# Start of an adaLN block kernel rebuilt: first batch's modulation rows by TensorE on all partitions, gates on 128 partitions, four groups half by half

## The chip, the cores and the metric

One core of a Trainium2 chip. The metric is the device time of one execution in microseconds (us). Five engines work side by side: TensorE (PE), VectorE (DVE), ScalarE (ACT), GpSimd (POOL) and SyncE (SP), which here only issues transfers.

## What is computed

x has 8 batches of 1024 tokens with 512 channels. Cut to what matters:

```python
mod = silu(c) @ wmod                      # (8, 6*512): sa, ca, ga, sb, cb, gb
ga = sign(ga) * max(|ga|, 0.25)           # the gates; gb likewise
h = layernorm(x) * (1 + ca) + sa
x = x + ga * attention(h)                 # attention output @ Wo.T + bo
h = layernorm(x) * (1 + cb) + sb
x = x + gb * ffn(h)                       # both operands quantised to FP6 in blocks of 32
```

The attention runs along axes such that only the first 16 of the 1024 tokens of each batch get a part that differs from token to token (128 "head" rows in all); for every other token it adds the row V = ga * bo. The kernel computes all tokens with x + V, and the head rows once more in full.

## The kernel before

**Tiling.** 16 groups of 512 tokens (two for each batch), each with 4 tiles of 128 tokens, so 64 tiles. The program of each engine is a loop over slots q = 0 to 63; slot q is one tile's product. Each engine's order is written out by hand: `due(q, lead)` says which group's step falls on slot q with a lead in slots, so that group g's statistics, modulation, maxima, scales and grid are made while the tiles of the groups before it are multiplied. Waits are semaphores with constants.

**A tile** (`product`, L579 to 597): TensorE turns four 128x128 blocks of the dequantised tile DD (L574), ScalarE rounds them to XH (L392), VectorE makes XL, what rounding left (L982). Then one matmul for the bias row (L587) and 12 of 512 columns: XH with the weights' high part WH (L591) and low part WL (L592), XL with WH (L596). VectorE adds the result to x (L1034), SyncE stores a group.

**A group** before that: x is loaded; V is added, on POOL for groups 0 and 1 (L320), by a DMA from DRAM that adds for the others (L313). ScalarE: sums (L419), squared deviations (L430), normalising into U (L408). POOL: times the row c = 1 + cb (L329), plus the row sb (L331). VectorE: block maxima (L1001), scales (L1006 to L1012), to the FP8 grid (L1020, two halves), back for the first half (L1027); POOL the second half (L340).

**Weights.** W is quantised once on VectorE (`quantise`, L751). For each batch POOL scales its rows by the gate (`scale_weights`, L354), TensorE turns them (L548), ScalarE and VectorE make WH (L398) and WL (L989). After the first batch one quarter is done in each of four slots (`FOLDS`).

**The start.** Six modulation products with 8 result rows, cE (8 batches) times a 512x512 piece of wmod (`modulation`, L525). The gates are computed on 8 partitions (`gate`, L773). Rows which all 128 partitions need (V, c, sb, the bias row in two parts) are written to the DRAM scratch and read back as broadcasts; ScalarE issues those of V, c and sb:

```python
act.wait_ge(v_row_done, 1)
act.dma_start(mod_dram[:, V, :], mrow[V]).then_inc(v_row_out, 16)
act.wait_ge(v_row_out, 16)
act.dma_start(v_bc[:], mod_dram[0:1, V, :].to_broadcast([P, D])).then_inc(v_in[0], 16)
```

VectorE's constants for the attention (temperatures, centred rows, centred diagonals BD at L792 to L796, rows LR at L804 and L806) all come before that. The slots of VectorE begin at -17, those of TensorE at 0.

**The head rows** (`head_work`, `attend`) ride in the slots: two norms and the modulation in slots 0 to 2, their three projections on TensorE in slots 5 to 7 (L672), three passes of attention from `BEGIN` = 8, each 15 slots, and the rest from `AFTER` = 50 on, up to slot 62.

## Time and profile before

| | |
|---|---|
| median of 3 runs | 385.32 us (383.96 to 385.49) |
| the profiled execution | 385.07 us, of which 382.8 are the span from first to last instruction |
| mean granted clock of TensorE | 0.938 of 2.4 GHz |
| busy: PE, DVE, ACT, POOL | 322.2, 290.9, 219.9, 233.8 us |
| moved by DMA | 68.10 MB, 178 GB/s on average |

Rows of the page give, for a group of like instructions, where in the kernel they stand (L591), engine, operation, what is written from what, shape and count, then busy time and the mean of one in ns, then the idle time of the engine just before them and what ended it. "PEclk" is the share of 2.4 GHz that TensorE was granted; 0.5 is its lower level of 1.2 GHz.

### The profile page before, as it was taken

The page shows a single profiled execution, that of the slowest core. Times are in us where ns is not written, and L with a number is a line of the kernel's source. Part 1 is how long each engine was busy: PE and PEld are TensorE (multiplying, and loading weights), DVE is VectorE, ACT ScalarE, POOL GpSimd, SP SyncE. Part 2 cuts the span into 40 slices and gives each one's busy share as a digit, 9 for nine tenths or more (in the row PEclk, how much of TensorE's full clock was granted, in tenths as well). Part 3 has the DMA queues.
Part 4 walks back from the last instruction along what each step waited for, and adds up shares of the span by engine and source line. Part 5 has one row for each costly group of instructions (what it writes and reads, how often), then busy time and mean ns, then how long its engine had stood idle before and what let it go on. Part 6 is the DMA issues. An engine that isn't in the chain of part 4 may idle for free.

```text
span 382.8 us, 6288 instructions
## 1 busy us (share of the span) xinstructions
PE 322.2 (84%) x2302; PEld 245.4 (64%) x2302; DVE 290.9 (76%) x500; ACT 219.9 (57%) x498; POOL 233.8 (61%) x139
## 2 busy tenths in 40 slices
PE   2950065886899999999999998989999999995994
PEld 0100012664799887778888776878887878674883
DVE  2893397598764698498969877999886799799533
ACT  2001858483755787688695968767874877120310
POOL 2004886929969569675995887596956693800100
PEclk9995569589999999999999999999998999999999
DMA  7998355869874966678486939684966971102032
GB/s 262 388 406 332 96 74 197 142 196 308 200 176 87 300 106 225 100 288 158 172 176 211 217 118 239 176 197 141 242 161 167 222 165 68 45 0 110 33 133 82
DMA packets 23156, 68.10 MB, mean 178 GB/s; under 512 B 2563, under 2 KB 2692, under 8 KB 19022
## 3 DMA queue, kind: packets, MB, share of 16 engines
q1 hardware_dynamic: 14982, 51.67, 37.9%
q0 software_dynamic: 7392, 14.68, 24.8%
q10 hardware_dynamic: 752, 1.36, 1.1%
q8 instruction: 18, 0.29, 0.3%
q14 instruction: 12, 0.10, 0.1%
HBM read 50.50 MB, written 17.20 MB: 177 GB/s over the span
## 4 chain that ended last, share of the span: by engine, by line
PE 49%; DVE 22%; issue 8%; ACT 7%; POOL 7%; DMA 4%; SPq 1%; DVEq 0%; POOLq 0%; ACTq 0%
PE ps L591 9%; PE ps L592 9%; PE ps L596 9%; PE ps L574 5%; PE ps L548 3%; DVE XL L982 3%; PE ps L672 3%; PE ps L587 3%; DMA v_bc<-mod_scratch 2%; POOL U L329 2%; POOL U L331 2%; DVE amax L1001 2%; DVE WL L989 2%; DVE X L1034 1%; PE ps L603 1%
## 5 line engine op out<-in xcount | busy, mean ns | idle before, releaser
L591 PE MATMUL ps<-WH,XH 128*128 128x512 f32 x256 | 103.0, 402 | 0.7 <-ACT XH L392 0.7
L592 PE MATMUL ps<-WL,XH 128*128 128x512 f32 x256 | 102.6, 401 | 0.0
L329 POOL TENSOR_TENSOR U<-U,c_bc 128x1024 f32<-128x1024 f32 x32 | 78.3, 2447 | 31.6 <-ACT U L408 31.6
L392 ACT ACTIVATE XH<-ps 128x512 fp32r<-128x512 f32 x64 | 37.9, 593 | 86.2 <-PE ps L574 86.1
L331 POOL TENSOR_TENSOR U<-U,sb_bc 128x1024 f32<-128x1024 f32 x32 | 76.8, 2398 | 2.5
L982 DVE TENSOR_TENSOR XL<-ps,XH 128x512 fp32r<-128x512 f32 x64 | 44.0, 688 | 45.1 <-ACT XH L392 42.5
L596 PE MATMUL ps<-WH,XL 128*128 128x512 f32 x256 | 69.7, 395 | 1.0 <-DVE XL L982 1.0
L408 ACT ACTIVATE U<-X,nmr,rstd 128x512 f32<-128x512 f32 x64 | 48.6, 810 | 21.0 <-DVE nmr L997 21.0
L592 PEld LDWEIGHTS ps<-WL,XH 128*128 128x128 f32 x256 | 49.5, 193 | 11.4
L419 ACT ACTIVATE unused<-X 128x512 bf16<-128x512 f32 x64 | 39.5, 620 | 29.6 <-POOL X L320 27.7
L596 PEld LDWEIGHTS ps<-WH,XL 128*128 128x128 f32 x256 | 48.5, 190 | 12.2 <-DVE XL L982 1.7
L591 PEld LDWEIGHTS ps<-WH,XH 128*128 128x128 f32 x256 | 49.8, 194 | 10.0 <-ACT XH L392 1.2
L1034 DVE TENSOR_TENSOR X<-ps,X 128x512 f32<-128x512 f32 x64 | 43.7, 682 | 9.9 <-PE ps L596 9.8
L340 POOL TENSOR_TENSOR DD<-Q,s 128x1024 f32<-128x1024 fp8e4 x16 | 30.7, 1916 | 32.8 <-DVE Q L1020 25.4
L430 ACT ACTIVATE unused<-X,negm 128x512 bf16<-128x512 f32 x64 | 45.6, 717 | 0.5
L1001 DVE TENSOR_REDUCE amax<-U 128x32 f32<-128x1024 f32 x32 | 38.7, 1211 | 4.8 <-POOL U L331 4.8
L574 PE MATMUL ps<-idf,DD 128*128 128x128 f32 x256 | 40.2, 283 | 0.2 <-POOL DD L340 0.2
L1020 DVE TENSOR_TENSOR Q<-U,ps 128x1024 fp8e4<-128x1024 f32 x32 | 39.0, 1218 | 0.6
L574 PEld LDWEIGHTS ps<-idf,DD 128*128 128x128 f32 x256 | 31.6, 146 | 3.2 <-issue 1.1
L587 PE MATMUL ps<-G,onesr 128*128 128x512 f32 x64 | 31.3, 489 | 0.9 <-DVE X L1034 0.9
L313 POOL DMA_DIRECT2D X<-mod_scratch x14 | 18.1, 1294 | 18.8 <-DMA X<-in_x 18.8
L320 POOL TENSOR_TENSOR X<-X,v_bc 128x1024 f32<-128x1024 f32 x4 | 9.2, 2341 | 31.4 <-DMA v_bc<-mod_scratch 31.4
(211 smaller groups left out, 441.8 us busy)
## 6 DMA issues: line engine op xcount, KB each, us to landing
X<-in_x SPq DMA_DIRECT2D x16, 1024.0 KB, 4.9
out<-X SPq DMA_DIRECT2D x15, 1024.0 KB, 7.6
X<-mod_scratch POOLq DMA_DIRECT2D x14, 1024.0 KB, 11.6
X<-in_wmod SPq DMA_DIRECT2D x4, 1024.0 KB, 9.4
c_bc<-mod_scratch SPq DMA_DIRECT2D x6, 256.0 KB, 9.9
sb_bc<-mod_scratch SPq DMA_DIRECT2D x6, 256.0 KB, 9.8
Wd<-in_w SPq DMA_DIRECT2D x1, 1024.0 KB, 12.7
U<-in_wmod SPq DMA_DIRECT2D x1, 1024.0 KB, 14.8
```

The costliest lines, as they stand in the source:

```text
L329: nc.gpsimd.tensor_tensor(a, a, spread(c_bc[:, b % 2, :]), ALU.mult).then_inc(u_done, 1)
L331: nc.gpsimd.tensor_tensor(a, a, spread(sb_bc[:, b % 2, :]), ALU.add).then_inc(h_done, 1)
L408: A.activation(U[:, g % 2, j, :], X1[:, g % XSLOTS, j, :], ACT.Identity, bias=nmr[:, g % 2, j:j + 1], scale=rstd[:, g % 2, j:j + 1]).then_ ...
L430: A.activation(unused[:, j % 2, :], X1[:, g % XSLOTS, j, :], ACT.Square, bias=negm[:, g % 2, j:j + 1], accum_out=ss[:, j:j + 1]).then_inc( ...
L574: m = TR(ps[:, XT_BANK + n % 2, c * P:(c + 1) * P], DD[:, j, c * P:(c + 1) * P], idf[:])
L587: M(bank, onesr[:], G2[:, b % 2, :], start=True, stop=False)
L591: M(bank, XH[:, n % 2, r], WH[:, b % 2, k, :], start=False, stop=False)
L592: M(bank, XH[:, n % 2, r], WL[:, b % 2, k, :], start=False, stop=False)
L596: m = M(bank, XL[:, n % 2, r], WH[:, b % 2, k, :], start=False, stop=k == NC - 1)
L982: TT(XL[:, n % 2, :], ps[:, XT_BANK + n % 2, :], XH[:, n % 2, :].bitcast(F32), ALU.subtract).then_inc(xl_done, 1)
L1001: RED(amax[:, h, :], blocks(U[:, g % 2, HALF * h:HALF * (h + 1), :]), AX, ALU.max, apply_absolute_value=True).then_inc(am_done, 1)
L1034: TT(a, ps[:, Y_BANK + n % 2, :], a, ALU.add).then_inc(o_done, 1)
```

## The change

What it does, part by part:

- **V.** TensorE makes the first batch's ga row on all 128 partitions at once (`spread`): the weights are one column of cE repeated 128 times. VectorE forms V from it with a broadcast of bo (`first_v`) and adds it to group 0 itself; POOL adds it to group 1. The c and sb rows of batch 0 come the same way; ScalarE copies them out of PSUM.
- **Gates.** Their 8 rows are turned into 128 partitions x 32 (4 chunks of 8 batches); the gate is computed there, and times bo and the bias as columns. Four blocks are turned back into 32 rows (gate-bias, V, gb, ga for 8 batches) and written to DRAM by one DMA. The bias row of a product is now picked out of G by the weights `pick`, so that no load for each batch is needed.
- **Head modulation.** ca and sa come from two products with 128 result rows in slots 0 and 1 (`head_rows`), read from PSUM; before, 8 broadcast loads.
- **Groups 0 to 3** (`FILLING`) are treated half by half, and both halves of DD are made by VectorE; their steps have slots of their own. The steps of group 0 stand before the loop.
- **Moved.** LR rows to slot 1 and BD's centring to slot 4 on VectorE; the product for the c rows of all batches to slot 0 on TensorE; head projections to slots 6 to 8, `BEGIN` to 9, `AFTER` to 51; the folds of batch b to slots 8b-5 to 8b-2.
- **Loads** are in another order: the first piece of wmod in two halves, the identity second, W before the second piece, BD and the head's x late. Three small loads go to ScalarE's queue. The DMA addition of V for group g+3 is issued after group g's modulation.

```diff
 def fold_slot(b, k):
-    return k if b == 1 else 56 + k if b == B else 8 * b - 8 + (0, 1, 4, 5)[k]
+    return 56 + k if b == B else 8 * b - 5 + k
...
+        NORMAL = {2: (3, 3), 3: (6, 6), 4: (8, 9)}
+        DEVIATE = {2: (2, 2), 3: (5, 5), 4: (7, 7)}
+        SUM = {2: (1, 1), 3: (4, 4), 4: (5, 6)}
+        FILLING = 3
...
             sp.dma_start(cTs[:], cT.rearrange("(k p) b -> p k b", p=P)).then_inc(c_loaded, 16)
-            load_mod(0)
+            sp.dma_start(idf[:], ident).then_inc(small_in, 16)
+            load_mod(0, 0, HALF)
+            load_mod(0, HALF, NC)
+            sp.dma_start(bo_bc, bo[None, :].to_broadcast([P, D])).then_inc(bo_in, 16)
             load_x(0)
+            sp.dma_start(Wd[:], w.rearrange("(c p) k -> p c k", p=P)).then_inc(w_in, 16)
             load_mod(1)
+            load_x(1)
             load_mod(2)
-            sp.dma_start(Wd[:], w.rearrange("(c p) k -> p c k", p=P)).then_inc(w_in, 16)
             load_mod(3)
-            load_x(1)
+            load_x(2)
+            sp.wait_ge(columns_cp, 1)
+            sp.dma_start(mod_dram[0:COLUMNS].rearrange("w b d -> (w b) d"), column_rows).then_inc(columns_out, 16)
...
         @block.gpsimd
+            add_attn_bias(1)
+            scale_weights(0, Wfirst, 0, HALF)
+            scale_weights(0, Wfirst, HALF, NC)
+            modulate(0)
+            sum_by_dma(2)
+            scale_weights(1, Wsecond)
+            sum_by_dma(3)
...
         @block.tensor
+            def spread(i, bank, signal):
+                for k in range(NC):
+                    pe.wait_ge(wmod_in[6 if i == 0 and k < HALF else i], 16)
+                    m = M(ps[:, bank, :], cE[:, k, 0:1].to_broadcast([P, P]), mod_w[i][:, k, :],
+                          start=k == 0, stop=k == NC - 1)
+                m.then_inc(signal, 1)
...
-                M(bank, onesr[:], G2[:, b % 2, :], start=True, stop=False)
+                M(bank, pick[:, b:b + 1].to_broadcast([P, P]), G[:], start=True, stop=False)
...
+                if q == 0:
+                    pe.wait_ge(c_heads, 1)
+                    pe.wait_ge(wt_low, NC)
+                    pe.wait_ge(rows_cp, 3)
+                    rows_of(2, LATE_ROWS)
+                    head_rows(4, CA_BANK)
+                elif q == 1:
+                    head_rows(5, SA_BANK)
...
         @block.vector
+            early_constants()
+            first_v()
+            dve.wait_ge(w_in, 16)
+            quantise(Wd[:, 0:HALF, :], Q8[:, 0], HALF * NB).then_inc(wd_done, 1)
+            gate(0, GA, BO, V, dve_step)
...
+            gate(1, GB, BIAS, GBIAS, gb_col)
+            scales(0)
+            quantise(Wd[:, HALF:NC, :], Q8[:, 1], HALF * NB).then_inc(wd_done, 1)
+            gate_bias_rows()
+            first_modulate()
+            maxima(0, 0)
+            block_scales(0, 0, 1)
+            to_grid(0, 0)
+            from_grid(0, 0)
+            for k in range(NC):
+                weight_low(0, k, W_FIRST_BANKS[k])
+            low_part(0)
```

Where the orders of the engines show it, with each instruction's semaphores. First TensorE at the start of the program, before (8x512 is a modulation with 8 result rows, L561 the gate turned, L548 the weights turned):

```order
L528 MATMUL ps<-X,cE 8x512 [waits wmod_in0,silu_done]
L555 MATMUL ps<-ones,lrow 128x1 [waits rows_ok,cleared]
L528 MATMUL ps<-X,cE 8x512 [waits wmod_in1]
L528 MATMUL ps<-X,cE 8x512 [waits wmod_in2]
L528 MATMUL ps<-U,cE 8x512 [waits wmod_in3]
L561 MATMUL ps<-idf,early 128x8 [waits gb_row,small_in]
L528 MATMUL ps<-X,cE 8x512 [waits wmod_in4,blq_cp]
L528 MATMUL ps<-Wb,cE 8x512 [waits wmod_in5,gb_cp]
L548 MATMUL ps<-idf,X 128x128 [waits mod_cp,wscaled]
```

and after (L589 is `spread`, L596 a modulation with 8 rows, L602 a gate turned, L639 the gate columns turned back, L623 the weights turned):

```order
L589 MATMUL ps<-X,cE 128x512 [waits wmod_in6,silu_done]
L589 MATMUL ps<-X,cE 128x512 [waits wmod_in0] x2
L596 MATMUL ps<-X,cE 8x512 [waits wmod_in0]
L602 MATMUL ps<-idf,msp 128x8 [waits rows_cp,small_in]
L596 MATMUL ps<-X,cE 8x512 [waits wmod_in1]
L602 MATMUL ps<-idf,msp 128x8 [waits rows_cp]
L589 MATMUL ps<-X,cE 128x512 [waits wmod_in2] x4
L639 MATMUL ps<-idf,TA 32x128 [waits gb_col]
L589 MATMUL ps<-U,cE 128x512 [waits wmod_in3] x4
L596 MATMUL ps<-U,cE 8x512 [waits wmod_in3,blq_cp]
L623 MATMUL ps<-idf,Wb 128x128 [waits g_rows,wscaled,columns_cp,v_row]
```

Three products with 128 result rows and two turns of the gates have come in; two of the six modulations have left for slots 0 and 1.

VectorE, after, from V on to the first turn's input (before, these steps lie in slots -17 to -2, with V and the gates on 8 partitions):

```order
L906 SCALAR_TENSOR_TENSOR v_bc<-odd,ps 128x512 [waits dve_step]
L911 TENSOR_TENSOR X<-X,v_bc 128x1024 [waits x_in0,v_row]
L862 TENSOR_REDUCE ps<-Wd 128x32 [waits w_in]
L890 TENSOR_SCALAR gate_sign<-ps 128x32 [waits gate_mm]
L1119 RECIPROCAL ps<-sd 128x4 [waits sd_done]
L917 CAST G<-ps 8x512 [waits columns_cp,cleared]
L959 SCALAR_TENSOR_TENSOR U<-ps,U 128x1024 [waits c_rows,z_done]
L962 TENSOR_TENSOR U<-U,ps 128x1024 [waits s_rows,u_first]
L1129 TENSOR_REDUCE amax<-U 128x32 [waits h_first]
L1155 TENSOR_TENSOR DD<-Q,ps 128x1024 [waits q_done]
L1114 TENSOR_TENSOR WL<-ps,WH 128x512 [waits wt_high] x4
L1107 TENSOR_TENSOR XL<-ps,XH 128x512 [waits xh_done]
```

The addition of V and the modulation of group 0's first half have moved from POOL to VectorE, and the low parts of the weights now stand behind the first half of DD.

## Rows read from the trace of the kernel before

**Rows 1.** The page, part 2: TensorE busy and its clock, in tenths

```profile
PE   2950065886899999999999998989999999995994
...
PEclk9995569589999999999999999999998999999999
```

**Rows 2.** Table by stage (us, busy us of each engine, clock, DMA share, GB/s)

```profile
0.00:69.02 69.02, 29.89 (x78) 8.88 (x78) 45.07 (x90) 27.84 (x68) 31.32 (x28) 0.78 0.75 250
69.02:128.31 59.29, 51.15 (x286) 42.63 (x285) 40.77 (x71) 33.45 (x81) 45.93 (x26) 0.91 0.77 192
128.31:374.80 246.49, 238.12 (x1931) 191.68 (x1930) 203.62 (x337) 158.58 (x350) 156.54 (x87) 0.99 0.59 157
374.80:382.80 8.00, 3.10 (x14) 2.24 (x12) 1.38 (x2) 0.00 (x0) 0.00 (x0) 1.00 0.31 98
...
80.00:90.00 10.00, 6.43 (x32) 4.82 (x30) 9.72 (x18) 5.07 (x14) 4.05 (x3) 1.00 0.88 291
```

**Rows 3.** Chain of waits before the first product (start us, us, what)

```profile
22.34 4.24 DMA mod_scratch<-early
26.60 7.60 DMA v_bc<-mod_scratch
...
36.63 2.35 POOL X L320
...
53.53 2.72 DVE XL L833
```

**Rows 4.** Timeline of TensorE: slot starts (start us, us, instruction)

```profile
69.02 0.79 PE L587 MATMUL ps<-G,onesr 128*128 128x512 f32 x1
...
98.02 0.48 PE L587 MATMUL ps<-G,onesr 128*128 128x512 f32 x1
...
128.31 0.48 PE L587 MATMUL ps<-G,onesr 128*128 128x512 f32 x1
```

**Rows 5.** Timeline of TensorE: modulation products

```profile
6.86 5.59 PE L528 MATMUL ps<-X,cE 128*8 128x512 f32 x8 [6.86 <-DMA X<-in_wmod]
...
21.43 3.60 PE L528 MATMUL ps<-U,cE 128*8 128x512 f32 x8 [1.09 <-DMA U<-in_wmod]
```

**Rows 6.** Groups of instructions by line (busy us, mean ns of one)

```profile
L329 POOL TENSOR_TENSOR U<-U,c_bc 128x1024 f32<-128x1024 f32 x32 | 78.3, 2447 | 31.6 <-ACT U L408 31.6
...
L408 ACT ACTIVATE U<-X,nmr,rstd 128x512 f32<-128x512 f32 x64 | 48.6, 810 | 21.0 <-DVE nmr L997 21.0
...
L982 DVE TENSOR_TENSOR XL<-ps,XH 128x512 fp32r<-128x512 f32 x64 | 44.0, 688 | 45.1 <-ACT XH L392 42.5 <-PE ps L596 2.5
...
L1020 DVE TENSOR_TENSOR Q<-U,ps 128x1024 fp8e4<-128x1024 f32 x32 | 39.0, 1218 | 0.6
L1001 DVE TENSOR_REDUCE amax<-U 128x32 f32<-128x1024 f32 x32 | 38.7, 1211 | 4.8 <-POOL U L331 4.8
...
L1027 DVE TENSOR_TENSOR DD<-Q,ps 128x1024 f32<-128x1024 fp8e4 x16 | 19.4, 1212 | 0.0
...
L354 POOL TENSOR_SCALAR Wb<-Wd,gbTs 128x512 f32<-128x512 f32 x24 | 16.2, 687 | 3.9 <-PE ps L672 3.9
...
L320 POOL TENSOR_TENSOR X<-X,v_bc 128x1024 f32<-128x1024 f32 x4 | 9.2, 2341 | 31.4 <-DMA v_bc<-mod_scratch 31.4
```

**Rows 7.** Timeline of VectorE: BD and LR constants

```profile
11.80 0.27 DVE L792 TENSOR_REDUCE bdm<-BD 128x1 f32<-128x128 f32 x1
...
17.00 0.68 DVE L806 TENSOR_TENSOR LR<-lrow,LR 1x512 fp32r<-1x512 f32 x1
```

**Rows 8.** Timeline of TensorE around its first slots [idle before]

```profile
66.52 1.09 PE L548 MATMUL ps<-idf,X 128*128 128x128 f32 x4 [4.68 <-DVE WL L989]
...
75.33 2.08 PE L596 MATMUL ps<-WH,XL 128*128 128x512 f32 x4 [1.03 <-DVE XL L982]
...
81.30 1.07 PE L596 MATMUL ps<-WH,XL 128*128 128x512 f32 x4
```

**Rows 9.** Timeline of TensorE: a head projection

```profile
104.54 3.73 PE L672 MATMUL ps<-sq,early 128*128 128x128 f32 x32
```

**Rows 10.** The page, part 6: DMA additions

```profile
X<-mod_scratch POOLq DMA_DIRECT2D x14, 1024.0 KB, 11.6
```

**Rows 11.** Timeline of POOL: a wait for x of group 3

```profile
85.87 1.29 POOL L313 DMA_DIRECT2D X<-mod_scratch  x1 [7.61 <-DMA X<-in_x]
```

More of the change, by code:

```diff
@@ L24, with build @@
 XSLOTS = 6
-V, C, SB, GB, GBIAS, CA, SA, GA, GBH, GBL = range(10)
-FIRST, LAST = -17, TILES * GROUPS
-BEGIN, PERIOD = 8, 15
-AFTER = 36 + 14
+GBIAS, V, GB, GA, C, SB = range(6)
+COLUMNS, ROWS = 4, 6
+LAST = TILES * GROUPS
+BEGIN, PERIOD = 9, 15
+AFTER = BEGIN + 2 * PERIOD + 12
 def fold_slot(b, k):
-    return k if b == 1 else 56 + k if b == B else 8 * b - 8 + (0, 1, 4, 5)[k]
+    return 56 + k if b == B else 8 * b - 5 + k
 FOLDS = {fold_slot(b, k): (b, k) for b in range(1, B + 1) for k in range(NC)}
-def build(nc, x, xh, WqT, WkT, WvT, WoT, bo, lna, BDs, rows, columns, masks, w, bias, cT, wmod, ident, out):
-    mod_dram = nc.dram_tensor("mod_scratch", (B, 10, D), F32, kind="Internal").ap()
+def build(nc, x, xh, WqT, WkT, WvT, WoT, bo, lna, BDs, rows, columns, masks, w, cT, wmod, ident, out):
+    mod_dram = nc.dram_tensor("mod_scratch", (ROWS, B, D), F32, kind="Internal").ap()
     xg = x.rearrange("b (g p j) d -> (b g) p j d", p=P, j=TILES)
@@ L183, in due, with additions, halves @@
             return g if r == 0 and 0 <= g < GROUPS else None
-        def mods(i):
-            return ps[0:B, (0, 1, 2, 3, 6, 7)[i], :]
+        def additions(g):
+            return g // XSLOTS + (g % XSLOTS >= 2)
+        NORMAL = {2: (3, 3), 3: (6, 6), 4: (8, 9)}
+        DEVIATE = {2: (2, 2), 3: (5, 5), 4: (7, 7)}
+        SUM = {2: (1, 1), 3: (4, 4), 4: (5, 6)}
+        def halves(q, early, lead):
+            done = [(g, h) for g, slots in early.items() for h in range(2) if slots[h] == q]
+            for h in range(2):
+                g = due(q, lead - h)
+                if g is not None and g > 4:
+                    done.append((g, h))
+            return done
+        FILLING = 3
         def pass_of(q):
@@ L374, in _ @@
             A = nc.scalar
+            act.dma_start(col[:], columns).then_inc(vec_in, 16)
+            act.dma_start(lrow[:], rows).then_inc(vec_in, 16)
+            act.dma_start(mk[:], masks).then_inc(mk_in, 16)
             act.wait_ge(c_loaded, 16)
@@ L411, in sums @@
             def sums(g, h):
[L412 to L413 removed]
+                if g == 0:
+                    act.wait_ge(v_row, h + 2)
+                elif g == 1:
+                    act.wait_ge(x1_done, h + 1)
                 else:
[L415 removed]
+                    act.wait_ge(x_added[g % XSLOTS], 16 * additions(g))
                 for j in range(HALF * h, HALF * (h + 1)):
@@ L511, in _ @@
                     weight_high(*FOLDS[q - 1], W_BANK)
+                if q == 0:
+                    deviations(1, 1)
+                    for h in range(2):
+                        normalise(1, h)
                 head_work(q)
-                for h in range(2):
-                    if (g := due(q, 9 - h)) is not None:
-                        normalise(g, h)
-                    if (g := due(q, 11 - h)) is not None:
-                        deviations(g, h)
-                    if (g := due(q, 13 - h)) is not None:
-                        sums(g, h)
+                if q == 1:
+                    copy_rows(c_rows_all, LATE_ROWS, 4, 1.0)
+                for g, h in halves(q, NORMAL, 9):
+                    normalise(g, h)
+                for g, h in halves(q, DEVIATE, 11):
+                    deviations(g, h)
+                for g, h in halves(q, SUM, 13):
+                    sums(g, h)
         @block.tensor
```

626 lines of the change are left out of this document (345 added, 281 removed).

## The prediction

> **What bounds the kernel now.** I read four views, in this order. The page's slices [rows 1] show where TensorE works: low and broken digits in the first seven or eight slices of 9.6 us, then mostly nines. The table by stage [rows 2] says it in numbers: before the first product, 69.02 us in which TensorE is busy for 29.89; then nine token tiles (slots 0 to 8, one product each) in 59.29 us; then 246.49 us with TensorE busy for 238.12 of them, at a granted clock of 0.99; the last slot and the tail take 8 us. A slot's floor on TensorE is the 3.43 us from 98.02 to 101.45 [rows 4] (a turn and one product with nothing beside them), so nine slots at the floor would take 31 us where these take 59. The change touches the first 128.31 us, and all it can save lies there.
>
> The chain of waits [rows 3] names what fills the first 69 us: the row v is written to DRAM (4.24 us) and read back on all partitions (7.60 us); POOL then adds it to tokens; DVE computes the second gate on 8 partitions after group 0's statistics, and at 53.53 rounds its bias row in a 2.72 us instruction of 8 partitions; POOL scales the weights; TensorE turns them. The slot starts [rows 4] are the measure that I carry over: 69.02, 98.02 (slot 4, the first of group 1) and 128.31 (slot 9).
>
> **Times at the new start, step by step.** I lay the new program's orders against the durations of rows, and look for when slot 0 starts.
>
> Loads. TensorE's first modulation starts when 1 MB is in, at 6.86; the one that starts at 21.43 waits for a load with 5.6 MB more in front [rows 5], so 0.385 MB/us or 2.7 us for each MB. The first half of the first weight piece is then in at about 5.7, the second at 7, x of group 0 at 10.5, W at 13.2, piece 2 at 16, x of group 1 at 18.6, piece 3 at 21.4, piece 4 at 24, x of group 2 at 27.
>
> TensorE. One modulation product with 512 columns costs 5.59 us when it begins at half rate and 3.60 at full rate [rows 5], 3.44 when the next follows at once. I take the same for 128 result rows as for 8, because in both the 512 columns are what streams. So: v on all partitions 5.7 to 11.5, gate rows 14.9, the first gate turned 16.3, piece 2 19.7, the second gate turned 21.3 (it waits for ScalarE, busy with deviations until 20.1 and then with the copy), the c rows 24.8, the four turns of the gate columns 25.4, sb rows 28.9, batch rows of sb 32.3, the turned weights 34.3.
>
> VectorE. v from 11.5 to 14.3 (four operations of 512 columns at 0.69), the two additions of group 0 to 16.7 (I take 1.2 each, as for L1020; POOL takes 2.45 for such an operation [rows 6]), half of W quantised to 21.0 (three passes over 1024 columns at 1.22 and two small ones), both gates to 23.6 (twelve operations of 32 columns, 0.2 each), the other half of W to 28.4, the bias rows 29.8, c and sb applied to half of group 0 32.3, maxima, scales, grid and back to 36.5, four low parts of the weights 39.1 [rows 6]. ScalarE's share beside it: sums and deviations of group 0 from 15.5 to 22.6, then its normalisation waits until 26.0 behind the copy of the turned gate columns, which itself waits for TensorE until 25.4; that wait is hidden, as VectorE is in W until 28.4. POOL's four weight scalings (0.69 each) end at 29.8, hidden too.
>
> Slot 0 therefore starts at about 39.1 in place of 69.02, with VectorE as the engine that sets it: 29.9 us earlier. Removed with it are the DRAM round trip of v and c (11.84 us of the chain) and the slow 8-partition operations on two SBUF operands beside POOL.
>
> On the round trip a page can be weighed. The rows give 4.24 and 7.60 us [rows 3], with loads of 1 MB in front of it in the same engines. The Trainium skill ("DMA: Bandwidth & Descriptors", section "Anatomy of one DMA") gives about 2.0 us fixed plus the bytes at 436 GB/s, an estimate of 2.0 and 2.6 us for these two; by that the removal would be worth 4.6 us and not 11.8. The trace disagrees, and my sum uses the new chain's own steps, so it doesn't hang on either.
>
> **The filling, slots 0 to 8.** What moves in: the batch rows of c and both head modulations, three products of 3.44 us on TensorE in slots 0 and 1 (10.3 us); on VectorE the centring of BD and the LR rows, which ran in 11.80 to 17.68 before [rows 7] (5.2 us without the two small ones), now in slots 1 and 4; and for groups 0 to 3 the second half of DD, 1.2 us a group, which POOL did.
>
> The clock: after an idle of 4.68 us TensorE's operations ran at half level from 66.52; four product steps at 75.33 took 2.08 us against 1.07 at 81.30 [rows 8]. The new start has a similar pause (34.3 to 37.9). I take half level for about 12.5 us as in the rows: the product of slot 0 costs 5.5, and the first moved modulation 2.8 more than at full rate.
>
> Then by hand, with the same durations and those 2.8 left out until the end: slot 0 from 39.1 to 44.7; two modulations to 51.6; slot 1 to 55.3; the third to 58.8; slot 2 to 62.8; slot 3 to 66.3; slot 4 at 67.8. There VectorE is behind: in slot 2 it must do 1.2 + 1.2 + 0.5 for group 1 and 3.6 for the head's second norm, in slot 4 3.0 for BD, beside 1.4 in every slot for the output addition and XL. So slot 5 is at 74 and slot 6 at 79; then slots 6, 7 and 8 are 7.5 us each, since TensorE has a head projection of 3.73 [rows 9] beside the floor and a weight turn: slot 7 at 86.4, slot 8 at 94, slot 9 at 100.9, and 103.7 with the 2.8. An operation of 512 columns that need not wait for the one before takes 0.60 in a row of them, as the piece at 45.06 [rows 3], and not 0.69; some 30 of these in the filling take 2.5 us off: 101.2. POOL (four passes of 2.4 us a group, 9.7 in about 17) keeps up.
>
> The DMA addition for group 5 now comes after group 2's modulation, at about 81, and by the row lands 11.6 us later [rows 10], at 93, when ScalarE would want it from about 90. I take 0 for it, since ScalarE's next urgent step is slot 9's, and keep 3 us for the upper end.
>
> **After slot 9.** Before, this is 254.5 us (128.31 to 382.80). The attention chain begins one slot later, so its first step (two products of 512 columns and four small ones, 1.9 us) now lies behind slot 9, and one more weight turn does, 0.4. The rest of the rhythm is the same: TensorE is busy 97% there. The folds are now in four slots in a row (8b-5 to 8b-2), before in slots 0, 1, 4, 5 of eight, whose VectorE share is heaviest (two grid passes); I take 0 between bounds of -3 and +3.
>
> Sum: 101.2 + 1.9 + 0.4 + 254.5 = 358.0 of span. The profiled execution was 385.07 with a span of 382.8, so 2.3 is added: 360.3, a gain of 24.8 on 385.07, which is 0.25 below the median of 385.32. A measurement of this kernel can tell about 0.5%, 1.9 us, from no change.
>
> **Rivals.**
> - *VectorE gives most of the filling back.* The moved constants and the head's norm delay XL, which delays every product; VectorE does 40.77 of 59.29 us in the filling before [rows 2] and gets about 9 more. If the moved work (10.3 on TensorE, 5.2 on VectorE, 3.6 for DD) hides nowhere, slots 0 to 8 take the old 59.3 plus 19.1 in place of 62.1: 377. Half of it hidden gives 367. Against it: the old 59.3 already holds pauses for weights and x.
> - *The start itself is late.* VectorE's list is in order, and it has about ten waits for other engines before slot 0, which I count at nothing; at 0.9 us each slot 0 starts at 48: 369. Against it: in the chain the read of v follows its write with nothing between (22.34 + 4.24 and 26.60) [rows 3], so the hops of the old start are small.
> - *Filling at TensorE's pace.* If VectorE's work fits beside it: 39.1 + 9 × 3.43 + 10.3 + 7.3 for two projections before slot 8's end, 3.7 for the third, and 1.7 of turns is 93: 352. For it: the old filling holds pauses that the new one need not have, as POOL's 7.61 us for x of group 3 [rows 11], whose load is issued earlier now.
> - *Slower: TensorE stays at half level through the filling and beyond.* Its place is the gaps that VectorE leaves in every slot; a product step then costs 0.43 and not 0.23, so a slot at least 3.0 us more. From 9 such slots on the 24.8 us are gone; 12 give 396. For it: half level lasted from 66.52 to 79 though TensorE was mostly busy. Against it: in the ten us behind, it was busy for only 6.43 and had full level throughout [rows 2].
>
> **How the numbers follow.** The forecast, 360.3, has 0.60; VectorE giving back (367) 0.15; the late start (369) 0.10; TensorE's pace (352) 0.12; slower (396) 0.03. The range goes from 350 to 372: below it takes in the third rival and -3 for the folds, above the first two with 3 us for ScalarE's wait. Faster by over 0.5%: 0.96; within: 0.01; slower: 0.03.
>
> **What would show it.** The first product's start at 37 to 42; v ready on all partitions by 15 with no DMA in its chain; no TensorE idle over 5 us after 6 us; slot 4 at 66 to 72, slot 9 at 98 to 104; from there on the same 250 to 258 us. Wrong would be a first product after 45, a span after slot 9 beyond 260, or a granted clock near 0.5 after slot 3.

## The result: 370.37 us, a gain of 14.8 where 24.8 were forecast

| | before | changed |
|---|---|---|
| median | 385.19 us | 370.37 us (369.68 to 372.18, 4 runs) |
| ratio | | 0.9628, 95% interval 0.9585 to 0.9672 |
| the profiled execution, span | 385.07, 382.8 | 371.03, 369.1 |
| slot 0 starts | 69.02 | 39.44 |
| slots 0 to 8 take | 59.29 | 68.31 |
| from slot 9 to the end of the span | 254.49 | 261.35 |

The kernel is faster, inside the range, and 10 us slower than the centre. The page of the changed kernel, its slices and its chain, against [rows 1]:

```profile
PE   3987999549999799989999999989999989995894
...
PEclk9999899997999999999999999999998999998999
...
PE 43%; DVE 36%; ACT 10%; issue 8%; DMA 1%; DVEq 0%; SPq 0%; ACTq 0%
```

Seven or eight slices of low digits before slot 0 and in the filling have shrunk to a few: after the first slice (of 9.2 us) come 9, 8, 7 and nines. A 5 and a 4 remain in the eighth and ninth slices (65 to 83 us), with a 7 in the clock right behind them. VectorE holds 36% of the chain that ended last. The table by stage, against [rows 2] (us from:to, length, busy us of PE, PEld, DVE, ACT, POOL, clock, DMA share, GB/s):

```profile
0.00:39.44 39.44, 28.32 (x86) 11.59 (x87) 30.54 (x70) 19.83 (x45) 18.70 (x23) 0.97 0.92 325
39.44:107.75 68.31, 58.64 (x296) 44.36 (x294) 52.24 (x91) 42.93 (x108) 38.56 (x22) 0.94 0.81 211
107.75:361.10 253.35, 240.70 (x1946) 193.46 (x1943) 206.60 (x345) 160.28 (x353) 159.66 (x88) 0.99 0.60 154
361.10:369.10 8.00, 3.10 (x14) 2.25 (x12) 1.39 (x3) 0.00 (x0) 0.00 (x0) 0.95 0.32 98
```

Before slot 0 TensorE does about what it did (28.32 us against 29.89), in 39 us instead of 69. Behind, both stages are longer than before. The chain of waits before the first product, against [rows 3] (start, us, what), has no transfer in it after the first piece of wmod:

```profile
1.79 4.29 DMA X<-in_wmod
...
6.21 5.50 PE ps L589 x8
...
14.00 0.70 DVE v_bc L906
14.72 2.36 DVE X L911 x2
...
28.21 0.68 DVE G L917
28.95 0.68 issue
29.63 1.23 DVE U L959
...
36.57 1.21 DVE WL L1114 x2
...
37.82 1.97 PE ps L660 x8
```

And the slot starts on TensorE's timeline (L675 is the bias row, L623 a weight turn; [idle before]), against [rows 4]:

```profile
39.44 0.78 PE L675 MATMUL ps<-G,pick 128*128 128x512 f32 x1
...
43.13 3.60 PE L596 MATMUL ps<-X,cE 128*8 128x512 f32 x8
...
66.64 0.50 PE L675 MATMUL ps<-G,pick 128*128 128x512 f32 x1 [0.65 <-DVE X L1162]
...
74.39 0.48 PE L675 MATMUL ps<-G,pick 128*128 128x512 f32 x1
...
82.96 0.45 PE L623 MATMUL ps<-idf,odd 128*128 128x128 f32 x1 [5.33 <-DVE WL L1114]
...
84.55 0.78 PE L675 MATMUL ps<-G,pick 128*128 128x512 f32 x1
...
107.75 0.47 PE L675 MATMUL ps<-G,pick 128*128 128x512 f32 x1
```

Slot 4 is at 66.64 and slot 5 at 74.39, where the forecast had 67.8 and 74 before it added its 2.8 us for half level at the start. Those 2.8 us were never paid: behind TensorE's pause before slot 0 the granted clock is 0.5 only until about 40.5, and the first moved modulation, at 43.13, runs at full rate. Then slot 6 is at 84.55 (79 forecast), and TensorE idles 5.33 us in front of it, waiting for VectorE. After that pause the same bias row takes 0.78 us and not 0.48: half level again. VectorE's timeline says what held it:

```profile
72.75 0.68 DVE L1114 TENSOR_TENSOR WL<-ps,WH 128x512 fp32r<-128x512 f32 x1
73.34 0.27 DVE L948 TENSOR_REDUCE bdm<-BD 128x1 f32<-128x128 f32 x1
73.65 0.15 DVE L949 TENSOR_SCALAR bdm<-bdm 128x1 f32<-128x1 f32 x1
73.84 5.19 DVE L952 TENSOR_SCALAR BD<-BD,bdm 32x32 f32<-32x32 f32 x4
...
79.58 1.19 DVE L952 TENSOR_SCALAR BD<-BD,bdm 32x32 f32<-32x32 f32 x4
...
80.93 0.69 DVE L1162 TENSOR_TENSOR X<-ps,X 128x512 f32<-128x512 f32 x1
```

and POOL's, over the same stretch:

```profile
74.07 2.39 POOL L370 TENSOR_TENSOR U<-U,c_bc 128x1024 f32<-128x1024 f32 x1
76.60 2.39 POOL L377 TENSOR_TENSOR U<-U,sb_bc 128x1024 f32<-128x1024 f32 x1
```

Four subtractions on 32x32 elements, the centring of BD, take 5.19 us, and end at 79.03, when POOL's modulation ends (78.99). The next four, with POOL's modulation over, take 1.19. One by one (the view of line L952: shortest, median and longest in ns), most take 0.23 to 0.27 us, and the one that starts at 74.17, just behind the start of a POOL pass, takes 2.32, about a whole pass:

```profile
L952 DVE TENSOR_SCALAR BD<-BD,bdm x8: 229/270/2320, 73.8 to 80.5; 32x32 f32<-32x32 f32 x8
```

The pair that starts at 76.53 takes 2.50, so two such waits and two ordinary subtractions make the 5.19 us. Not every VectorE instruction beside POOL waits: the sum at 73.34 and the 128x1 product at 73.65 have both ends in SBUF as well and take the 0.27 and 0.15 us that they took before.

In the kernel before the subtractions stood at 12.29, and POOL had no instruction there; that row lies between the two of [rows 7], from which the 3.0 us were sized (timeline of VectorE, kernel before):

```profile
12.29 1.03 DVE L796 TENSOR_SCALAR BD<-BD,bdm 32x32 f32<-32x32 f32 x4
```

The slower price could have been read in the kernel before. The same step of the gate there (L779, on 8 partitions, SBUF to SBUF) stands once where POOL is silent and once beside POOL's first modulation pass (46.07 to 48.41):

```profile
19.75 0.41 DVE L779 TENSOR_SCALAR hs<-hs 8x512 f32<-8x512 f32 x1
...
46.40 2.29 DVE L779 TENSOR_SCALAR hs<-hs 8x512 f32<-8x512 f32 x1
```

The prediction also uses two rows of the kernel before that it does not show. The piece at 45.06 in the chain of waits, and the slot start at 101.45 on TensorE's timeline, are these:

```profile
45.06 0.60 DVE hs L777
```

```profile
101.45 0.48 PE L587 MATMUL ps<-G,onesr 128*128 128x512 f32 x1
```

So the missing 10 us are mainly in two places: slots 5 and 6, 19.4 us where 12.4 were forecast, and slots 10 to 15, 30.8 us where the kernel before took 27.1. The rest is spread thinly over slots 16 to 63.

### The profile page after: what moved, and what is told of

Its sections match the earlier page's. It is cut to its first block, busy times and chain, and to the rows that moved or that the text cites. A ratio compares the mean times of both kernels' runs of the same rounds, so it can differ in the third digit from the quotient of the medians.

```text
span 369.1 us, 6369 instructions
## 1 busy us (share of the span) xinstructions
PE 330.8 (90%) x2334; PEld 251.7 (68%) x2334; DVE 290.8 (79%) x508; ACT 223.0 (60%) x505; POOL 216.9 (59%) x131
## 4 chain that ended last, share of the span: by engine, by line
PE 43%; DVE 36%; ACT 10%; issue 8%; DMA 1%; DVEq 0%; SPq 0%; ACTq 0%
PE ps L679 7%; PE ps L680 7%; PE ps L684 7%; DVE XL L1107 5%; PE ps L660 4%; DVE Q L1148 4%; DVE WL L1114 3%; DVE amax L1129 3%; ACT U L447 3%; PE ps L763 3%; DVE X L1162 3%; PE ps L623 3%; DVE DD L1155 3%; ACT XH L430 2%; ACT unused L460 2%
## 5 line engine op out<-in xcount | busy, mean ns | idle before, releaser
L370 POOL TENSOR_TENSOR U<-U,c_bc 128x1024 f32<-128x1024 f32 x31 | 75.6, 2439 | 48.3 <-ACT U L447 48.2
L430 ACT ACTIVATE XH<-ps 128x512 fp32r<-128x512 f32 x64 | 37.8, 591 | 84.8 <-PE ps L660 84.6
L377 POOL TENSOR_TENSOR U<-U,sb_bc 128x1024 f32<-128x1024 f32 x31 | 74.1, 2389 | 4.5 <-POOL U L370 0.2
L684 PE MATMUL ps<-WH,XL 128*128 128x512 f32 x256 | 68.8, 390 | 0.0
L460 ACT ACTIVATE unused<-X 128x512 bf16<-128x512 f32 x64 | 39.4, 617 | 0.1
L356 POOL TENSOR_TENSOR DD<-Q,s 128x1024 f32<-128x1024 fp8e4 x12 | 23.0, 1916 | 23.4 <-DVE Q L1148 21.8
L675 PE MATMUL ps<-G,pick 128*128 128x512 f32 x64 | 31.3, 490 | 0.6 <-DVE X L1162 0.6
L346 POOL DMA_DIRECT2D X<-mod_scratch x14 | 18.5, 1325 | 17.5 <-DMA X<-in_x 12.7
L389 POOL TENSOR_SCALAR Wb<-Wd,TA 128x512 f32<-128x512 f32 x28 | 18.9, 691 | 12.8 <-PE ps L623 8.3
## 6 DMA issues: line engine op xcount, KB each, us to landing
X<-mod_scratch POOLq DMA_DIRECT2D x14, 1024.0 KB, 12.8
```

Of the source, the lines that this page charges most:

```text
L370: nc.gpsimd.tensor_tensor(a, a, spread(c_bc[:, b % 2, :]), ALU.mult).then_inc(u_done, 2 if g == 0 else 1)
L377: nc.gpsimd.tensor_tensor(a, a, spread(sb_bc[:, b % 2, :]), ALU.add).then_inc(h_done, 2 if g == 0 else 1)
L460: A.activation(unused[:, j % 2, :], X1[:, g % XSLOTS, j, :], ACT.Identity, accum_out=total[:, j:j + 1]).then_inc(sum_done, 1)
L684: m = M(bank, XL[:, n % 2, r], WH[:, b % 2, k, :], start=False, stop=k == NC - 1)
```

## The experiments

Each ratio is against the kernel before on the same chip. The table gives where the time lay, in us, from TensorE's slot starts; "5+6" is slot 5's start to slot 7's, "10-15" slot 10's to slot 16's.

| kernel | ratio [95%] | slot 0 at | 5+6 | slots 0-9 | 10-15 | 10-62 |
|---|---|---|---|---|---|---|
| before | 1 | 69.02 | 14.0 | 64.0 | 27.1 | 241.8 |
| changed | 0.9628 [0.9585, 0.9672] | 39.44 | 19.4 | 73.7 | 30.8 | 248.0 |
| changed, again | 0.9610 [0.9567, 0.9654] | 40.08 | 17.7 | 73.1 | 30.7 | 247.4 |
| no_centre | 0.9484 [0.9428, 0.9540] | 41.24 | 12.3 | 67.6 | 32.3 | 249.3 |
| centre_act | 0.9472 [0.9402, 0.9543] | 41.38 | 12.8 | 67.2 | 30.8 | 246.5 |
| centre_q1 | 0.9600 [0.9543, 0.9657] | 41.29 | 11.3 | 68.9 | 32.4 | 252.7 |
| warm | 0.9693 [0.9639, 0.9747] | 41.25 | 16.8 | 71.2 | 30.7 | 250.5 |
| fold_old | 0.9701 [0.9655, 0.9748] | 41.58 | 19.4 | 74.5 | 29.9 | 247.7 |
| b_shift | 1.0026 [0.9995, 1.0057] | 68.98 | 14.0 | 62.8 | 27.4 | 244.2 |
| swap | 0.9645 [0.9605, 0.9684] | 40.0 | 17.5 | 72.7 | 32.3 | 249.3 |
| centre_act_swap | 0.9517 [0.9468, 0.9566] | 40.42 | 11.3 | 65.6 | 32.3 | 249.2 |
| a_shift10 | 0.9537 [0.9496, 0.9579] | 40.31 | 17.6 | 70.6 | 28.4 | 247.6 |
| centre_act_shift10 | 0.9392 [0.9357, 0.9427] | 40.20 | 11.3 | 63.7 | 28.4 | 246.5 |
| roundtrip | 1.0009 [0.9975, 1.0043] | 53.01 | 19.7 | 74.0 | 30.7 | 247.8 |

The ratio rests on 4 to 10 runs of each kernel; the slots are those of the one execution that was profiled, and for no_centre and centre_q1 that was the slowest (367.99 and 372.92 us, medians 365.81 and 369.63). Some of the table moves without an edit. With the same program up to slot 0 it starts at 39.4 to 41.6. Slot 13 takes 5.4 us in both executions of the changed kernel, in centre_act, warm and roundtrip, and 6.9 to 7.0 in no_centre, centre_q1, swap and centre_act_swap, whose edits do not touch it. In the two executions of the changed kernel slots 32 to 39 take 36.5 and 38.1 us, and slots 32 to 47 together 73.4 and 72.8.

The changed kernel once more, on the chip of centre_q1, b_shift and roundtrip:

> The changed kernel once more, beside the three others of this call, as their common base: 370 to 373 us. In the last call slot 0 started at 41.2 to 41.6 in four kernels whose start is the same program as here, where it was 39.44; there the second piece of wmod came in at 18.1 and TensorE waited. If that is the run and not the kernel, this one too may start anywhere from 39.4 to 41.6.

It came at 370.38 us: the difference between the two kernels repeats. The four subtractions take 5.18 us there and again end with POOL's pass.

### The centring of BD: left out, given to ScalarE, or moved to slot 1

Without the subtractions (no_centre; this kernel leaves the centring out, so its attention is not the right one):

```diff
-                    for q in range(4):
-                        r = slice(32 * q, 32 * q + 32)
-                        link(TS(BD[r, i, r], BD[r, i, r], bdm[r, n:n + 1], None, ALU.subtract))
```

> BD is not centred (the eight 32x32 subtractions of L952 are left out, so the logits use uncentred projections); the rest of the changed kernel is as it was. Theory A: these eight small instructions cost VectorE 6.4 us in slot 4 because the first four sat behind POOL's modulation (5.19 us against 1.03 us for the other kernel), TensorE idled 5.3 us for it and came back at half rate; then slots 5 and 6 (10.16 and 9.21 us) fall to about 5 and 7.5, and the time falls by 5 to 8 us, to 362 to 365. Rival B: VectorE is behind in the filling anyway (its list for groups 1 and 2), and the wait reappears in slots 5 to 7: under 2 us, 368 to 370.

Measured 365.81 us (364.46 to 367.99), ratio 0.9484, 0.8 us above theory A's range and 2.2 below rival B's; slots 5 and 6 fell from 19.4 (17.7 in the repeat) to 12.3, close to the 12.4 of the forecast.

The eight subtractions on ScalarE (centre_act), while VectorE keeps only the sums and means:

```diff
+                elif q == 6:
+                    act.wait_ge(bd_mean, 2)
+                    for n, i in enumerate((0, 2)):
+                        for j in range(4):
+                            r = slice(32 * j, 32 * j + 32)
+                            A.activation(BD[r, i, r], BD[r, i, r], ACT.Identity, bias=bdm[r, n:n + 1]
+                                         ).then_inc(bd_done, 1)
```

> The same centring, but the eight 32x32 subtractions are done by ScalarE in slot 6 (as an addition of minus the mean), VectorE keeps only the sums and means. Theory A (VectorE's two-sided small instructions wait for POOL): ScalarE's take 0.2 us each also while POOL modulates, 1.6 us in all in a slot where it idles, so the gain is that of leaving them out, within 1 us: 362 to 366. Rival B: any engine's access slows beside POOL, then these eight take over 0.5 us each and XH of slot 7 is late: 367 or more.

Measured 366.61 us (363.49 to 369.44), ratio 0.9472, slots 5 and 6 in 12.8. ScalarE's timeline of this kernel, and that of POOL beside it:

```profile
83.93 2.70 ACT L520 ACTIVATE BD<-BD,bdm 32x32 f32<-32x32 f32 x8
```

```profile
80.82 1.28 POOL L346 DMA_DIRECT2D X<-mod_scratch  x1
```

Eight take 2.70 us, 0.34 each where 0.2 was expected, in about the place where VectorE needed 5.19 + 1.19. POOL's next modulation starts at 88.33, so this run does not show how ScalarE fares beside it, and does not decide between theory A and rival B; it shows that the work costs next to nothing there. Computing all and leaving the centring out give the same time within their intervals: the loss in slots 5 and 6 was this step on VectorE.

The same subtractions on VectorE, at the end of its slot 1 (centre_q1):

```diff
                 elif q == 1:
                     bias_rows()
+                    centre_diagonals()
...
-                elif q == 4:
-                    centre_diagonals()
```

> The centring of BD stays on VectorE, with the same instructions, but moves from slot 4 to the end of slot 1, where POOL has nothing between 57.6 and 69.2. Theory A: each group of four small instructions takes 1.03 us there, as in the kernel before, not 5.19; slots 5 and 6 fall to 12 to 13 us together from 19.4, slots 1 to 3 grow by up to 3: a gain of 3 to 6 us on the changed kernel of this call. Rival: the slowness belongs to the instructions (32 partitions, 32 columns) or to VectorE's place in the order, then slot 1 grows by 6 and nothing is gained.

VectorE's timeline of this kernel; POOL's last instruction there had ended at 59.41:

```profile
60.91 1.04 DVE L952 TENSOR_SCALAR BD<-BD,bdm 32x32 f32<-32x32 f32 x4
...
62.49 1.04 DVE L952 TENSOR_SCALAR BD<-BD,bdm 32x32 f32<-32x32 f32 x4
```

Same engine, same instructions, 1.04 us where they took 5.19: what makes them slow is POOL's work beside them. Slots 5 and 6 fell to 11.3. But the time fell only to 369.63, 0.8 us under the changed kernel beside it where 3 to 6 were expected: slots 1 to 3 grew by 4.1 to 4.8 (expected up to 3). The profiled execution, 3.3 us above the median, also has longer slots 10 to 15 and 32 to 39. Of this kernel's expected gain only the local part came.

### TensorE kept busy through the pause

```diff
+                elif q == 5:
+                    for n in range(20):
+                        M(bb, onesr[:], LR[:, 0, :], start=True, stop=True)
```

(Nothing reads these 20 products.)

> Twenty matmuls of 512 columns with no use are put on TensorE behind slot 5's product, into a PSUM bank that is free there; the centring stays on VectorE. They fill 4.6 of the 5.3 us in which TensorE idles at 77.6 to 83. Theory C: of the loss in slots 5 and 6 about 2 to 3 us are the half rate that follows the idle; slot 6 falls from 9.21 to about 7 and the time by 2 us, to 368. If the half rate cost nothing (VectorE was late for slot 7 anyway), the time stays at 370 to 371, with slot 7 starting where it did.

TensorE's timeline of warm:

```profile
79.24 4.72 PE L784 MATMUL ps<-LR,onesr 128*128 128x512 f32 x20
84.77 0.30 PE L623 MATMUL ps<-idf,odd 128*128 128x128 f32 x1 [0.80 <-DVE WL L1117]
...
85.58 0.47 PE L675 MATMUL ps<-G,pick 128*128 128x512 f32 x1
```

The bias row takes 0.47 instead of 0.78, and slot 6 takes 7.43 instead of 9.21. From the first turn behind the pause to slot 7 it is 8.24 us (84.77 to 93.01) against 10.80 (82.96 to 93.76). So the half level after the pause cost 2.5 us of those 19.4; in the repeat of the changed kernel, where the same stretch takes 9.84, it cost 1.6. The total did not fall: it is 373.42 us, 3 more than the changed kernel. In the profiled executions 1.8 of that is a later slot 0 (41.25 against 39.44), which the edit does not touch, and slots 32 to 39 took 39.3 against 36.5 and 38.1. The expected gain of the whole is a miss, and only the local one stands.

### The folds where they were before

```diff
-    return 56 + k if b == B else 8 * b - 5 + k
+    return 56 + k if b == B else k + 3 if b == 1 else 8 * b - 8 + (0, 1, 4, 5)[k]
```

> The weight folds of batches 2 to 7 go back to slots 8b-8 + (0, 1, 4, 5); nothing else. The stretch behind slot 10 takes 6.2 us longer in the changed kernel than in the one before. Theory D: the folds in four slots in a row cause it (VectorE's two grid passes and the fold in the same slot): then 3 to 6 us come back, 364 to 367. Rival E: it is the attention chain, shifted by one slot against the groups' rhythm: then under 1.5 us either way, 369 to 372.

Measured 374.45 us, ratio 0.9701, above the ranges of both theories. Slots 10 to 62 take 247.7 against 248.0 us, with slots 10 to 15 0.9 shorter. Four folds in a row are not what made the later part longer. At the old places the kernel is about 4 us slower; in the profiled executions half of that is a later slot 0 (41.58 against 39.44), before any of these folds, so how much the folds cost is not shown.

### The attention one slot later in the kernel before

```diff
-BEGIN, PERIOD = 8, 15
+BEGIN, PERIOD = 9, 15
...
-AFTER = 36 + 14
+AFTER = 37 + 14
```

(with the two steps behind `AFTER` that would leave the last slot drawn in by one.)

> The kernel before, with the attention passes begun one slot later (BEGIN 9, AFTER 51, the last two steps of the head rows in the same slots as before): nothing else. Theory E: the attention chain, one slot later against the groups' four-slot rhythm, puts its heavy VectorE steps on slots that are already heavy; then slots 10 to 63 take 3 to 6 us longer than the 241.8 us of the kernel before, and the time rises to 388 to 391. Rival: the stretch is longer in the changed kernel for another reason (order on POOL, the four folds in a row); then this stays at 384.5 to 386.5.

Measured 386.31 us, ratio 1.0026, inside the rival's range; slots 10 to 15 in 27.4 against 27.1. The shift by itself does not cost the 3.7 us. This kernel has the attention in the same slots as the changed one, so it is the better measure for them: slot by slot the changed kernel is longer by 2.45 us in slot 12 (6.33 against 3.88), by 0.5 in slots 11 and 14 each, and within 0.05 in the three others.

### V through DRAM again

```diff
+            act.dma_start(v_dram, v_first[0:1, :]).then_inc(wv_in, 16)
+            act.wait_ge(wv_in, 16)
+            act.dma_start(v_bc[:], v_dram.to_broadcast([P, D])).then_inc(wv_in, 16)
...
-                STT(v_bc[:], gate_tmp, 2.0, m, ALU.mult, ALU.mult).then_inc(v_row, 1)
+                STT(v_first[:], gate_tmp, 2.0, m, ALU.mult, ALU.mult).then_inc(bd_done, 1)
+                dve.wait_ge(wv_in, 32)
```

> In the changed kernel VectorE's row V goes out to DRAM from one partition (2 KB) and comes back as a broadcast to 128 partitions (256 KB) before anything uses it, as in the kernel before; all else stays. By the rows of the kernel before (4.24 and 7.60 us behind the loads) slot 0 starts 10 to 12 us later and the time rises by about as much, to 381 to 384. By the page's 2.0 us and 2.6 us it is 4.6 us: 375 to 377. Rival: VectorE takes no step while it waits, so nothing hides it; only if the quantising of W were moved into the wait would it be less.

Measured 385.74 us, ratio 1.0009 [0.9975, 1.0043]: this one step takes the whole gain of the change back, more than the 381 to 384 that were expected. Slot 0 starts at 53.0, 12.9 us later than in the changed kernel beside it. The chain of waits of this kernel, and what VectorE waits for on its timeline:

```profile
14.26 0.69 DVE v_first L912
14.95 10.21 issue
...
25.26 4.52 DVE X L919 x2
```

```profile
25.17 0.06 DVE L914 MEMSET dn<- 128x1 f32 x1 [10.22 <-DMA v_bc<-v_scratch]
```

VectorE stands for 10.21 us, close to the 11.84 that [rows 3] gave and far from the 4.6 that was estimated from the Trainium skill ("DMA: Bandwidth & Descriptors", "Anatomy of one DMA"). That section of the Trainium skill gives its figures for a transfer that GpSimd's queue issues. Here ScalarE issues both (at 15.04 and 19.07), so the 4.6 us were borrowed from another path, and neither this run nor [rows 3] is a test of them. The two additions behind it now coincide with POOL's own on group 1 and take 4.52 us instead of 2.36; POOL's two take 6.67 where they took 4.67. That is 10.2 + 2.2 of the 12.9 us.

### The order of loads

```diff
-            sp.dma_start(Wd[:], w.rearrange("(c p) k -> p c k", p=P)).then_inc(w_in, 16)
             load_mod(1)
+            sp.dma_start(Wd[:], w.rearrange("(c p) k -> p c k", p=P)).then_inc(w_in, 16)
```

> Only the order of the two loads changes, the centring stays in slot 4. Theory: 0 to 1.5 us under the changed kernel's 370.4, slot 0 at 39 to 40, with slots 5 and 6 at 17.7 to 19.4 together as before.

> Centring on ScalarE as in centre_act, and the second piece of wmod is loaded before W and not behind it. The second piece is then in 2.7 us earlier (15.4 at the latest instead of 18.1), before TensorE is free for it at 16.3, and W 2.7 us later at worst at 18, against VectorE's need at 17. Theory: slot 0 starts at 39 to 40 in every execution and not at 41.2, and the time is 364 to 366, 4.5 to 6 us under the changed kernel's 370.4. Rival: W comes in late at 18 and more and the start only swaps one wait for another; then slot 0 stays at 41 and the time at centre_act's 366.6.

Neither shows a gain: swap 371.82 us (0.9645 against 0.9610 for the changed kernel, intervals that overlap; 368.9 to 370.4 were expected), centre_act_swap 366.06 (0.9517 against 0.9472). Slot 0 starts at 40.0 and 40.4, inside the range that it has without the edit, so one execution of each decides nothing about the start.

### The attention one more slot later in the changed kernel

```diff
-BEGIN, PERIOD = 9, 15
+BEGIN, PERIOD = 10, 15
```

> The changed kernel with the attention passes begun in slot 10 and not 9; nothing else. Slots 10 to 16 take 30.8 us in the changed kernel and 27.1 in the one before; a shift of that one by a slot left them at 27.4. Theory F: VectorE has no gap between 114.2 and 133.8 there because the attention's norm steps of pass 0 (slots 11 and 12) meet group 3's steps, which are half by half and all on VectorE; one slot later they meet group 4's lighter slot, and slots 10 to 16 change by over 1 us either way. Rival G: the load of VectorE is simply more than these slots hold, wherever the steps stand; then slots 10 to 17 stay within 1 us of the same sum, and the time at 369 to 373.

Measured 367.73 us, ratio 0.9537, under the 369 to 373 of rival G. Slots 10 to 15 fell from 30.8 to 28.4, as theory F had it. But most of that is where the count begins and ends. The attention's first step has left slot 9 (5.40 us before the shift, 3.42 behind it) for slot 10, and a slot of 7.0 us has moved from 15 to 16. From slot 10 to slot 17, the stretch that rival G names, it is 35.5 against 34.7 us, within G's 1 us, so that only the time speaks against G. Over slots 9 to 16, which take in both moves, it is 38.9 against 40.1 us, 1.2 less. Slots 16 to 31 take 74.5 where they took 71.6, and slots 10 to 62 as long as before (247.6 against 248.0 and 247.4). From slot 9 to slot 63 the gain is 1.8 us against the repeat and 2.3 against the first execution. What fills slots 10 to 15 shows in the table by stage over just these six slots, of the kernel before,

```profile
133.03:160.14 27.11, 27.11 (x258) 21.22 (x257) 21.21 (x39) 19.83 (x46) 19.90 (x13) 1.00 0.62 148
```

of the changed kernel, with its slot 12,

```profile
121.28:127.61 6.33, 4.04 (x25) 3.20 (x23) 6.09 (x13) 6.01 (x14) 4.19 (x2) 1.00 0.74 168
...
113.15:143.91 30.76, 28.48 (x242) 22.62 (x240) 26.18 (x45) 21.48 (x50) 21.43 (x14) 1.00 0.56 131
```

and of a_shift10:

```profile
110.95:139.39 28.44, 27.06 (x154) 22.52 (x152) 27.10 (x47) 20.28 (x49) 20.46 (x13) 1.00 0.59 147
```

The third busy figure is VectorE's: 21.21 us before, 26.18 after. In slot 12 TensorE stands for 2.3 of 6.33 us. On its timeline VectorE has no gap from 114.2 to 137 us of the changed kernel. A piece of it:

```profile
121.61 1.22 DVE L1155 TENSOR_TENSOR DD<-Q,ps 128x1024 f32<-128x1024 fp8e4 x1
122.75 1.21 DVE L1129 TENSOR_REDUCE amax<-U 128x32 f32<-128x1024 f32 x1
123.88 0.68 DVE L989 TENSOR_REDUCE ps<-sq 128x16 f32<-128x512 f32 x1
...
125.37 0.68 DVE L1107 TENSOR_TENSOR XL<-ps,XH 128x512 fp32r<-128x512 f32 x1
```

and TensorE's next turn of a weight:

```profile
126.79 0.63 PE L623 MATMUL ps<-idf,Wb 128*128 128x128 f32 x4 [2.29 <-DVE WL L1114]
```

TensorE waits here for WL, the fold's low part (125.96 to 126.64), which stands right behind XL; both stand behind two passes of 1.2 us and the attention's norm. Over the six slots VectorE makes three DD passes where it made one, three grid passes instead of two, five maxima instead of four, and one more low part: four passes, 1.1 us each from start to start, and one of 0.6 account for the 5.0 us more that it is busy. In a_shift10 VectorE has as much to do (27.10 us) and 1.3 us of gaps instead of 4.6, and TensorE's waits for WL there are 0.67 and 0.71 us instead of 2.29. So in slot 12 VectorE, full, makes TensorE stand, and where the attention's norm falls among its passes changes by about 0.9 us what is lost. Nothing was run with less work on VectorE in these slots, so that its extra passes cause the 3.4 us is argued from the wait and the busy times and not shown.

### Both edits together

```diff
-BEGIN, PERIOD = 9, 15
+BEGIN, PERIOD = 10, 15
```

on centre_act.

> The two edits that each made the changed kernel faster, in one kernel: the subtractions on ScalarE (ratio to the kernel before 0.947 alone) and the work between slots begun one slot later (0.954 alone; the changed kernel itself 0.961). Theory H: they remove different waits, the first VectorE's stall beside GpSimd in slot 5, the second a part of the full VectorE in slots 10 to 16. Then slots 5 to 7 stay near 12 us and slots 10 to 16 fall from 31 to 28 or 29, and the ratio is 0.934 to 0.943 (360 to 363 us against 385). Theory I: both only give VectorE room in the same stretch, slots 4 to 16, and what the first gives the second cannot give again; then the ratio is that of the first alone, 0.944 to 0.952, and slots 10 to 16 stay at 30 or more.

Measured 362.08 us (360.39 to 363.39, 6 runs), ratio 0.9392 [0.9357, 0.9427]: every number of theory H came. Its page:

```profile
PE   3889799779999899989999999889999997995994
...
PEclk9999899999999999999999999999999999999898
```

Slots 5 and 6 take 11.3 us, slots 10 to 15 28.4. The two gains do add, but H's reason for the second is not borne out: slots 10 to 62 take 246.5 us as in centre_act, and what the shift gives lies in slot 9 (3.43 against 5.41). The rest between these two profiled executions is a slot 0 that starts 1.2 us earlier and slots 5 and 6, 11.3 against 12.8, which the shift does not touch. Slot 9 starts at 100.4, where the forecast had 101.2, and the time is 1.8 us above the forecast. This is the fastest of all kernels here.

## Why the prediction was right, and 10 us too good

**The start, right.** Slot 0 was put at 39.1 and came at 39.44; V was ready at 14.7 (forecast 14.3), the two additions of group 0 ended at 17.08 (16.7), W's second half at 28.3 (28.4), the four low parts of the weights at 38.96 (39.1); TensorE starts to turn the tiles when two of them are there, at 37.8. The chain named VectorE as the engine that sets it, which it is. The rival of a late start is out.

**The round trip, right by the row.** The sum has no term for it, as the new chain has no such step, but the prediction said that 11.84 us go with it. Put back, it makes VectorE stand for 10.21 us and the kernel 15.4 us slower than the changed kernel beside it (385.74 us against 370.38).

**The filling up to slot 4, right, and in part by luck.** Slot 4 came at 66.64 (67.8, or 70.6 with the 2.8), and no wait for the group 5 addition was found on the path. But "half level for about 12.5 us as in the rows" did not come: it lasted 2.7 us from TensorE's first instruction behind the pause, at 37.82. Slot 0's product took 3.7 us and not 5.5, and the 2.8 for the first moved modulation were not paid. Without these 4.6 us the forecast has slot 9 at 96.6, and 107.75 is then 11 us late and not 6.5. The sum's error is so much larger than its result shows: 7.0 in slots 5 and 6, 1.6 in slot 4 (7.75 us against 6.2), and the 2.5 us taken off for operations that need not wait, which no slot shows by itself.

**"In slot 4 3.0 for BD" failed.** The step sized it from [rows 7], where POOL is silent, and slot 4 lies where POOL modulates. It took 7.6 us, from 73.34 to 80.9; TensorE idled 5.33 us for it and resumed at half level (2.5 us by warm). Slots 5 and 6 took 19.4 us and not 12.4, which alone is more than the error of the filling (68.3 against 62.1), and no_centre, centre_act and centre_q1 each remove it. The prediction itself spoke of "slow 8-partition operations on two SBUF operands beside POOL" as something that the change removes, and did not ask which new ones it puts there. Nor are two SBUF operands needed: the subtraction reads one tensor and a column of means, and L779 of the kernel before reads a single tensor (0.41 us against 2.29). The Trainium skill has the rule ("SBUF — State Buffer", section "Terms"): VectorE and GpSimd arbitrate for one port pair, exclusive for a full instruction, and the loser blocks altogether. The trace agrees for these subtractions: single ones of 2.32 us, as long as a pass, and 5.19 us for four that end with POOL's pass, against 1.04 with POOL idle. It does not bear it out for every VectorE instruction: the sum of 0.27 us at 73.34 ran beside a pass.

**"The rest of the rhythm is the same" failed.** After slot 9 the sum added 2.3 us to 254.5, and 261.4 were measured. Against b_shift, which has the attention in the same slots, 3.4 us more lie in slots 10 to 15, 2.45 of them in slot 12. The sum charged the 1.2 us a group for DD's second half to slots 0 to 8 alone, and the table by stage shows VectorE with 5.0 us more in slots 10 to 15, where it has no room. It never asked what VectorE does in the slots in which the last half-by-half group and the attention's first norm meet. The folds, 0 between -3 and +3, are confirmed at 0 for the later part.

**VectorE gives back filling** (367, 0.15) was the rival nearest to what happened, but not for its reason: it was not the sum of the moved work, but one small step with a wait in it, and a full stretch behind slot 9. TensorE's pace, with slot 9 at 93, was out of reach: even with both repairs it starts at 100.4. Four things stood outside what the prediction set as its signs, although the time fell into its range: slot 9 (107.75, set at 98 to 104), an idle of TensorE over 5 us (5.33), a span after slot 9 beyond 260 (261.35), and a clock near 0.5 after slot 3 (82.96 to about 88.3).

**Open.** Why the gains of centre_q1 and warm in slots 5 and 6 were lost again further on is not settled: slots 32 to 47 take 76.5 and 75.7 us in their profiled executions and 73.4 and 72.8 in the two of the changed kernel, and no edit touches them; b_shift shows the same against the kernel before (75.5 against 72.6). One profile of each does not tell an effect from the spread. Nor was it tried to leave group 3 to be treated whole, which would show what VectorE's 5 us more cost in slots 10 to 15.

## What to carry to other kernels

Before a step is moved, look up what the neighbouring engine does in the new place: a price read where POOL was silent does not hold where POOL streams, and eight tiny instructions stood in a step of 7.6 us, more than two products at the floor. The old trace may hold the price already, at another line of the same kind. When extra work is charged to the stage that is being rebuilt, count VectorE's busy time also in the slots behind it: here TensorE stood for 2.29 us in a slot in which VectorE had no gap. When steps are moved by a slot, take a stretch wide enough to hold them before and after. Two small repairs (the centring on ScalarE, the attention one slot later) added up: 0.9610 to 0.9392.

## What the runs showed of the hardware

- Some VectorE operations with input and output in SBUF wait for POOL: single subtractions of 32x32 took up to 2.32 us, four of them 5.15 to 5.22 in seven executions, against 1.03 to 1.20 with POOL not modulating; two additions of 128x1024 took 4.52 against 2.36. POOL pays too: its two additions took 6.67 us beside those, 4.67 without. A sum over BD (128x128 to 128x1) did not wait: 0.27 us beside POOL and without it.
- Eight 32x32 operations on ScalarE, with POOL not modulating, took 2.70 us.
- The length of a pause does not by itself say at which level TensorE comes back. It was half level after 5.33 us (bias row 0.78 us against 0.48), and full level after 0.80 us (0.47). In the repeat of the changed kernel TensorE came back from 3.70 us at full level and fell to half level 0.8 us later (to about 88.3), and after pauses of 1.82 and 1.23 us, which in the first execution left it at full level, it was at half level (bias row 0.78).
- A row of 2 KB written to DRAM and read back as 256 KB took 10.21 us with loads of 1 MB under way: 4.0 from the issue of the write to that of the read, 6.1 from there.
